# A q/k/v projection stage: head sums of squares in pairs, variance and root one and two groups later

## What is computed

```python
q = silu(short_conv_1d(x @ Wq + bq, q_conv)).reshape(B, S, h, d)
q = q / (norm(q, axis=-1, keepdims=True) + 1e-06)      # 16 heads of 32
k = silu(short_conv_1d(x @ Wk + bk, k_conv)).reshape(B, S, h, d)
k = k / (norm(k, axis=-1, keepdims=True) + 1e-06)
v = silu(short_conv_1d(x @ Wv + bv, v_conv)).reshape(B, S, h, d)
alpha = sigmoid(x @ Wa + ba)
beta = sigmoid(x @ Wb + bb)
out_gate = silu(x @ Wg + bg)
```

## Time and profile before

| | us |
|---|---|
| median of three runs | 3616.78 (3613.68 to 3622.12) |
| the profiled execution | 3620.39 |
| its span, first to last instruction | 3618.7 |
| TensorE busy | 3316.4 (92%) |
| DVE busy | 2785.5 (77%) |
| ScalarE busy | 1577.6 (44%) |
| GpSimd busy | 1849.7 (51%) |

### The profile page before, as it was taken

One profiled execution on the slowest core, in us unless ns is written; L12 is line 12 of the kernel. 1 busy time (PEld: TensorE's weight loads), 2 busy tenths in 40 slices (PEclk: granted clock), 3 DMA queues, 4 the chain that ended last, 5 costly groups with the idle time before them and its releaser, 6 DMA issues. The chain is left out here.

```text
span 3618.7 us, 193662 instructions
## 1 busy us (share of the span) xinstructions
PE 3316.4 (92%) x83728; PEld 2771.6 (77%) x83728; DVE 2785.5 (77%) x4487; ACT 1577.6 (44%) x2332; POOL 1849.7 (51%) x1724
## 2 busy tenths in 40 slices
PE   6999997899999999996999999999995886999999
PEld 4888885576767676765999999999995764888887
DVE  6767675787878787875888888888887866776765
ACT  3554543577777777670111111111112332455454
POOL 2232322565565656654777777777774431323232
PEclk9999998899999999997999999999997997999999
DMA  2221213132323232226666666666665773212121
GB/s 107 79 104 70 104 70 128 45 100 72 106 75 97 84 97 84 85 75 170 188 187 186 189 189 185 188 187 188 187 186 172 225 232 116 100 73 104 70 104 58
DMA packets 494532, 458.34 MB, mean 127 GB/s; under 512 B 55952, under 2 KB 458000, under 8 KB 474640
## 3 DMA queue, kind: packets, MB, share of 16 engines
q1 hardware_dynamic: 494480, 457.69, 40.9%
HBM read 336.97 MB, written 120.60 MB: 126 GB/s over the span
## 5 line engine op out<-in xcount | busy, mean ns | idle before, releaser
L274 POOL TENSOR_TENSOR ffn_out<-ffn_gate,ffn_xres 128x512 f32<-128x512 f32 x128 | 177.7, 1418 | 790.5 <-DVE ffn_gate L235 790.1
L660 DVE SCALAR_TENSOR_TENSOR ain_conv<-ain_padded,ain_taps,ain_conv 128x512 f32<-128x512 f32 x384 | 416.4, 1084 | 13.6
L1287 ACT ACTIVATE rec_yf<-rec_ps_f 128x256 f32<-128x256 f32 x129 | 49.5, 384 | 639.2 <-DVE rec_f_t L1218 639.2
L761 POOL TENSOR_TENSOR ain_conv<-ain_conv,ain_term 128x512 f32<-128x512 f32 x192 | 272.1, 1417 | 16.0
L1102 POOL TENSOR_TENSOR rec_d_norm<-rec_dmat,rec_early 128x512 f32<-128x512 f32 x131 | 166.5, 1271 | 210.1 <-DVE rec_dmat L1168 210.1
L46 PE MATMUL ffn_ring<-ffn_mixrh,ffn_wrh 128*128 128x512 f32 x512 | 214.9, 420 | 20.1 <-DVE ffn_mixrl L180 20.1
L816 ACT ACTIVATE ain_buf<-ain_conv 128x512 f32<-128x512 f32 x192 | 120.9, 630 | 232.6 <-POOL ain_conv L761 147.2
L46 PE MATMUL ffn_ring<-ffn_mixkh,ffn_wkh 128*128 128x512 f32 x512 | 216.3, 422 | 0.0
L1327 PE MATMUL rec_ps_scores<-rec_qk_pe,rec_kb 32*32 32x64 f32 x8320 | 144.3, 217 | 66.7 <-issue 45.4
L46 PE MATMUL ffn_ring<-ffn_mixrh,ffn_wrl 128*128 128x512 f32 x512 | 202.0, 395 | 0.0
L46 PE MATMUL ffn_ring<-ffn_act_h,ffn_wvh 128*128 128x512 f32 x512 | 201.8, 394 | 0.0
(11 more groups left out here) (234 smaller groups left out, 10337.8 us busy)
## 6 DMA issues: line engine op xcount, KB each, us to landing
rec_early<-coeffs SPq DMA_DIRECT2D x532, 128.0 KB, 2.8
rec_qkv<-streams SPq DMA_DIRECT2D x130, 384.0 KB, 3.2
streams<-ain_buf SPq DMA_DIRECT2D x48, 1024.0 KB, 5.1
rec_qk_pe<-streams SPq DMA_DIRECT2D x131, 256.0 KB, 3.0
rec_late<-coeffs SPq DMA_DIRECT2D x520, 64.0 KB, 1.9
rec_k_in<-streams SPq DMA_DIRECT2D x133, 128.0 KB, 2.9
ffn_x<-in_x SPq DMA_DIRECT2D x16, 1024.0 KB, 8.4
ffn_xres<-in_x SPq DMA_DIRECT2D x16, 1024.0 KB
```

Of the source, the lines that this page charges most:

```text
L274: last = nc.gpsimd.tensor_tensor(out[:, m, :], gate[:, m, :], xres[:, m, :], ALU.add)
L660: nc.vector.scalar_tensor_tensor(out=out[:], in0=pad[:, n:n + TOK], scalar=taps[:, u // KT, u % KT, n:n + 1], in1=out[:], op0=ALU.mult, op ...
L761: nc.gpsimd.tensor_tensor(out[:], out[:], term[:], ALU.add).then_inc(pool_conv, 1)
L1287: nc.scalar.activation(yf[:, 1], ps_f[:, :, 1, :], ACT.Copy).then_inc(f2_ready, 1)
```

## The change

The head sums no longer follow groups 5 to 12 one by one. They come in pairs: sums 0 and 1 behind group 6, 2 and 3 behind group 8, 4 and 5 behind group 11, 6 and 7 behind group 13. `var` of the next tile moves from behind group 7 to behind group 8. On ScalarE the root moves from ahead of `silu(10)` to ahead of `silu(11)`, behind two gates.

```diff
--- before.py
+++ after.py
@@ -844,13 +844,13 @@
                         deviation(t + 1)
                     if more and u == 10:
                         high(t + 1, 1 - s)
-                act.wait_ge(heads_summed, 8 * t + 8)
-                nc.scalar.activation(inv_norm[HROWS, :], ps_rows[HROWS, :], ACT.Sqrt).then_inc(rooted, 1)
                 silu(t, 10, more)
                 act.wait_ge(gate_stored, 16 * t)
                 act.wait_ge(w_split["g"], 1)
                 for m in range(KT):
                     if m == 2:
+                        act.wait_ge(heads_summed, 8 * t + 8)
+                        nc.scalar.activation(inv_norm[HROWS, :], ps_rows[HROWS, :], ACT.Sqrt).then_inc(rooted, 1)
                         silu(t, 11, more)
                     act.wait_ge(group_done, 16 * t + 12 + m + 1)
                     nc.scalar.activation(gate[:, m, :], ring[m][:], ACT.Silu, bias=bias[:, 3, m:m + 1]).then_inc(gate_ready, 1)
@@ -898,6 +898,8 @@
                     pe.wait_ge(rooted, t)
                 nc.tensor.matmul(ps_rows[:], head_sum[:, n, :], sq[:, n % 4, :], start=(n == 0),
                                  stop=(n == 7)).then_inc(heads_summed, 1)
+
+            SUMS_AFTER = {6: (0, 1), 8: (2, 3), 11: (4, 5), 13: (6, 7)}
 
             def slot(t, s, more):
                 pe.wait_ge(x_low, t + 1)
@@ -915,11 +917,12 @@
                     else:
                         pe.wait_ge(biased, 12 * t + u - 3)
                     product(nc, ring[u % 4][:], *W["qkvg"[j]], m, xh[s], xl[s]).then_inc(group_done, 1)
-                    if u == 5:
+                    if u == 6:
                         pe.wait_ge(heads_selected, 1)
-                    if 5 <= u < 13:
-                        head_sums(t, u - 5)
-                    if more and u == 7:
+                    if u in SUMS_AFTER:
+                        for n in SUMS_AFTER[u]:
+                            head_sums(t, n)
+                    if more and u == 8:
                         var(t + 1)
                     if more and u == 11:
                         spread_rstd(t + 1)
```

## The result

The changed kernel took 3679.15 us (median of four runs, 3676.46 to 3684.3) against 3619.1 us before in the same comparison: ratio 1.0167, 95% interval 1.0155 to 1.0179. The forecast was 3682 in a range of 3658 to 3693, and slower. The profiled execution's span is 3676.1 us.

A forecast was written before the change was run, and what follows sets the result against it. A DVE, ScalarE and GpSimd chain containing norms was taken as the bound, not TensorE. Terms 3.84 + 0.37 + 0.42 = 4.63 us, times 14 tiles = 65 us, on 3616.8 gave 3682 us, range 3658 to 3693.

The forecast's parts named there:

- The loop: In the q/k/v stage, a chain through DVE, ScalarE and GpSimd containing norms sets the 61.14 us tile period; TensorE runs beside it.
- The root: On ScalarE, moved behind the silu of unit 10 and two gates, it delays DVE's norms by 3.84 us a tile.
- GpSimd's convolution of unit 8: Three of its instructions come beside DVE's convolution of unit 9: +0.42 us a tile, half of the bound 0.84.
- L678: DVE instruction in norms, now starting inside GpSimd's last add: +0.37 us a tile, bounds 0 and 0.37.
- The end of the stage: After the last tiles, counted at nothing, bounds -1 and +2 us, as norms there already waited 1.77 us for the root.
- The variance one group later: On TensorE, behind group 8: costs nothing; if the cover were gone, one group, 3.2 us.
- The late `silu(11)`: On ScalarE, the silu of unit 11 moves from 1025.56 to about 1026.4, hidden by the wait for centre.
- rival 3: On ScalarE, the table load brings a further 1.38 us: 19 us more, 3701 us; chance 0.03.
- Rival 2: On DVE, the normalisation's 2.35 us earlier start reaches low: each tile loses only 1.5 us, 3638 us; chance 0.04.
- Rival 1: TensorE is the bound; removing 3.1 us of its waits a tile makes the kernel faster, 3574 us; chance 0.05.

The follow-up runs named there:

- the spread alone: Kernel before the change, with only the spread of the reciprocal deviations put ahead of head sum 6, behind group 11: 3626.86 us, ratio 1.0025.
- the doubled group: Kernel before the change, with group 5 of each tile computed twice into the same buffer, 12 matmuls more on TensorE: 3624.24 us, ratio 1.0012.
- centre_first: Kernel before the change, with centre of tile t + 2 ahead of norms of tile t on DVE, and its mean behind group 13 on TensorE: 3601.3 us, ratio 0.9955.

## Why the prediction was right

**The loop.** That TensorE's 94% busy is not the bound held: 12 matmuls more in it a tile cost 0.09 us of period, and its removed waits gained nothing. That `norms` lies in the loop held: the root's delay appears in the period nearly one to one (3.75 us of wait, less 0.07 for a shorter L678, +3.60 in the period), and two thirds of it vanish when `centre` goes first.

**The terms.** The root: 3.84 us predicted, 3.75 measured, the gates following `silu(10)` 0.1 us sooner. GpSimd's convolution of unit 8: +0.42 taken between 0 and 0.84, 9.17 - 8.61 = +0.56 measured. Of the three instructions counted, the multiply and the last add grew; the first add (1029.59, 1.29 us) did not. The prediction read the Trainium skill's rule (SBUF — State Buffer, Who interferes with whom), that whoever issues first has the shared ports for its whole instruction and the other blocks, as giving the upper bound of 0.84. The trace does not reach it: the first add was as long as before, with DVE's convolution beside it. L678: +0.37 predicted, 0.72 - 0.81 = -0.09 measured. Together 3.75 + 0.56 - 0.09 = 4.22, against 4.12 in the period and 4.63 predicted; no row places the 0.1 us left over. The end of the stage, taken at nothing within -1 and +2 us, cost 59.3 - 14 x 4.12 = 1.6 us.

By the period 14 x 0.51 = 7 us too much was predicted, and the profiled span is 7.6 us under 3618.7 + 65. That the median of 3682 is only 3 us high is partly luck: the kernel before had 3619.1 in this comparison, not the 3616.8 that the forecast starts from, and the runs of the changed kernel spread over 8 us. The +0.42 was half of a bound, not a reading, and its error (0.14 too low) works against that of L678 (0.46 too high).

**The step that failed**, without changing the outcome, is "I take all of it, since the situation is the same" for L678. It was not the same: the length of L678 hangs on how much of GpSimd's instruction is left when it starts. Four cases from the kernels before and after, DVE's L678 and GpSimd's instruction under way. After the change, tile 5: 1046.08 + 0.72 = 1046.80, behind an add that ended at 1045.23 + 1.29 = 1046.52. After, last tile:

```profile
1681.10 1.47 DVE L678 TENSOR_SCALAR ain_inv_norm<-ain_inv_norm 32x512 f32<-32x512 f32 x1 [3.75 <-ACT ain_inv_norm L853]
```

```profile
1681.00 1.29 POOL L761 TENSOR_TENSOR ain_conv<-ain_conv,ain_term 128x512 f32<-128x512 f32 x1
```

Before, tile 5, GpSimd beside L678 at 1021.30 to 1022.11:

```profile
1020.92 0.91 POOL L758 TENSOR_SCALAR ain_term<-ain_padded,ain_taps 128x512 f32<-128x512 f32 x1 [0.21 <-POOL ain_conv L761]
```

Before, last tile, beside L678 at 1620.73 to 1621.91:

```profile
1620.34 1.29 POOL L761 TENSOR_TENSOR ain_conv<-ain_conv,ain_term 128x512 f32<-128x512 f32 x1
```

GpSimd's instructions end at 1046.52, 1682.29, 1021.83 and 1621.63, L678 at 1046.80, 1682.57, 1022.11 and 1621.91: each time 0.28 us behind. The other tiles of the two kernels give 0.27 to 0.29. From the earlier trace rows, the add of 1024.24 ends at 1025.52, so L678 should have been put at 1025.80, 0.66 us after its start, and the term at -0.15.

**The covers.** The variance one group later cost nothing that a row shows. The late `silu(11)` cost nothing on the loop while `norms` was on it; with `centre` first, where ScalarE closes the loop, it is 0.75 of the 1.17 us. The table load brought no drain: it ends at 1044.16 + 1.28 = 1045.44 and the root starts at 1045.46, so rival 3 and the figure of the Trainium skill behind it (ScalarE: Activation LUTs, What ACT_TABLE_LOAD costs) are not borne out for this case. Rival 2 fell with the spread alone: the 2.35 us did not reach `low`, whose wait for ScalarE grew from 0.38 to 1.95 us. (Its loss of 1.5 us a tile is 3.84 - 2.35 and leaves out the two smaller terms; with them it would have been 2.3.) Rival 1 fell with the doubled group.

**Seen in the profile as listed:** the period 65.4 (65.8 expected, from 61.14; 65.9 from 61.25), the wait at L678 in 16 tiles, no wait at L636, TensorE idle for 6.8 us a tile (7 expected).

## What to carry to other kernels

The busiest engine at 94% can still be beside the loop; walk back from one tile's start to the last's by who waited for whom, and price a moved step by whether it sits in time an engine would have waited anyway or ahead of a queue that others wait for. A root with two table loads was free in ScalarE's idle 4.5 us and cost 3.75 us a tile behind it, because DVE's next `centre` is queued behind its reader. And when a step only feeds stores, like `norms` here, put it behind the step that the next tile waits for; here that made the kernel 16 us faster.

## What the runs showed of the hardware

Two things were not expected. DVE's L678, a tensor_scalar from SBUF to SBUF, ended 0.27 to 0.29 us behind the end of GpSimd's instruction under way in all 32 tiles of the kernels before and after, where it starts about 0.10, 0.38 or 0.85 us behind that instruction; so its length there (0.71 to 1.47 us) measures GpSimd's phase. It is not a rule without exception. In `centre_first` L678 starts 0.07 us behind GpSimd's multiply; in seven tiles L678 takes 0.42 us and ends ahead of the multiply, which takes 0.97:

```profile
1016.32 0.42 DVE L678 TENSOR_SCALAR ain_inv_norm<-ain_inv_norm 32x512 f32<-32x512 f32 x1
```

```profile
1016.25 0.97 POOL L759 TENSOR_SCALAR ain_term<-ain_padded,ain_taps 128x512 f32<-128x512 f32 x1 [0.21 <-POOL ain_conv L762]
```

In seven others of the same run, with nearly the same offset, L678 takes 0.89 or 0.90 us and the multiply 0.69 or 0.70.

And an engine's wait for another can hold a third engine's work apart: with 2.35 us of DVE's wait removed, GpSimd's multiply grew from 0.69 to 0.91 us and its add from 1.27 to 1.59, and the kernel got 8 us slower.
